# The last feed-forward in pairs of tiles, laid between the attention's steps, with its normalisations on GpSimd

## The reference

```
x += tanh(g) * masked_attention(x_normalised, ctx)            # layer 0, stage A
x += tanh(g) * quantised_gated_ffn(x_normalised)              # layer 0, stage B
q, k, v = h @ Wq.T + bq, ctx @ Wk.T + bk, ctx @ Wv.T + bv     # layer 1, stage C, 16 heads
probs   = softmax(where(mask, clip(q k / 4, -50, 50), -10000 then clipped))
delta   = residual_scale * ((probs v) @ Wo.T + bo)
x      += tanh(g) * (layernorm(delta) * gamma + beta)
x      += tanh(g) * ((silu(h @ Wgate.T) * (h @ Wup.T)) @ Wdown.T)   # layer 1, stage D, 1024 hidden
```

## Time and profile before

| | |
|---|---|
| median of three runs | 264.27 us |
| profiled execution, its own time | 264.11 us |
| span of its instructions | 262.3 us |
| PE, DVE, ACT, POOL busy | 212.0, 181.0, 132.8, 83.9 us |
| stage C from about 127 us, stage D alone from about 196 us | |

### The profile page before, as it was taken

The page is one execution under the profiler, slowest core; times in us unless marked ns, Lnnn a source line. Parts: engine busy times, 40 slices in busy tenths (PEclk is TensorE's granted clock), DMA queues, the critical chain, the costliest instruction groups (busy, mean ns, idle before and its releaser), DMA issues.

```text
span 262.3 us, 4538 instructions
## 1 busy us (share of the span) xinstructions
PE 212.0 (81%) x1658; PEld 174.5 (67%) x1658; DVE 181.0 (69%) x457; ACT 132.8 (51%) x296; POOL 83.9 (32%) x108
## 2 busy tenths in 40 slices
PE   0285557979889889897798688775999999999992
PEld 0264325858778778786576466654877888888882
DVE  2769879598988988786428999998984333262333
ACT  1138874478667667679755455553322323222220
POOL 2301111175856856868505333442100000000000
PEclk9999955699999999999959999997999999999999
DMA  5999003900000000000000000000000000020002
GB/s 169 369 390 301 5 0 139 343 1 0 2 0 0 2 1 0 2 2 0 0 2 2 0 2 4 0 4 0 2 2 0 0 0 2 0 80 2 0 0 80
DMA packets 9238, 12.55 MB, mean 48 GB/s; under 512 B 1025, under 2 KB 7937, under 8 KB 9217
## 3 DMA queue, kind: packets, MB, share of 16 engines
q1 hardware_dynamic: 8784, 12.07, 13.3%
q10 hardware_dynamic: 432, 0.20, 0.4%
HBM read 11.22 MB, written 1.05 MB: 47 GB/s over the span
## 4 chain that ended last, share of the span: by engine, by line
PE 50%; DVE 27%; ACT 7%; DMA 6%; issue 4%; POOL 3%; SPq 1%; DVEq 0%; ACTq 0%; POOLq 0%
PE PB L1259 16%; PE PB L1278 7%; DMA WRAW<-w_dram 6%; PE PB L1073 6%; PE PB L1172 4%; PE PB L1085 3%; DVE XV L524 3%; PE PB L1108 2%; PE PB L1112 2%; DVE HBQ L742 2%; PE PB L1019 2%; DVE RD L728 2%; DVE HBQ L572 2%; ACT SIL L906 2%; DVE HSD L578 2%
## 5 line engine op out<-in xcount | busy, mean ns | idle before, releaser
L1259 PE MATMUL PB<-SGN,WHI 128*128 128x512 f32 x128 | 40.5, 397 | 0.0
L1073 PE MATMUL PB<-SGN,XQH 128*128 128x512 f32 x64 | 27.7, 433 | 1.3 <-DVE XQL L553 1.3
L699 DVE TENSOR_TENSOR WRAW<-WRAW,PB 128x512 f32<-128x512 f32 x16 | 11.0, 686 | 24.0 <-ACT WRAW L993 23.9
L1278 PE MATMUL PB<-WHI,SGN 128*128 128x256 f32 x128 | 25.6, 283 | 2.2 <-DVE SGN L707 1.8
L1073 PE MATMUL PB<-SGN,XQL 128*128 128x512 f32 x64 | 27.1, 424 | 0.0
L289 POOL TENSOR_TENSOR RSTD<-MVS,MHALF 128x1 f32<-128x1 f32 x24 | 13.4, 560 | 40.9 <-DVE MVS L401 40.9
L1259 PEld LDWEIGHTS PB<-SGN,WHI 128*128 128x128 f32 x128 | 22.9, 188 | 4.5 <-issue 0.2
L1259 PE MATMUL PB<-SGN,WLO 128*128 128x512 f32 x64 | 25.2, 394 | 0.0
L993 ACT ACTIVATE WRAW<-PB 128x512 f32<-128x512 f32 x16 | 9.6, 600 | 28.0 <-PE PB L1259 28.0
L1278 PEld LDWEIGHTS PB<-WHI,SGN 128*128 128x128 f32 x128 | 20.7, 188 | 3.6 <-DVE SGN L707 2.4
L316 POOL TENSOR_TENSOR HBQ<-HBQ,HR 128x512 f32<-128x512 f32 x16 | 17.6, 1098 | 17.2 <-DVE HR L590 17.2
(11 more groups left out here) (122 smaller groups left out, 545.7 us busy)
## 6 DMA issues: line engine op xcount, KB each, us to landing
WRAW<-w_dram SPq DMA_DIRECT2D x2, 2048.0 KB, 12.1
X<-x_dram SPq DMA_DIRECT2D x2, 512.0 KB, 5.8
CTXT<-ctxt_dram SPq DMA_DIRECT2D x1, 1024.0 KB, 9.6
CTX<-ctx_dram SPq DMA_DIRECT2D x1, 1024.0 KB, 12.0
WRAW<-w_dram SPq DMA_DIRECT2D x1, 1024.0 KB, 14.9
...
```

What stands on the lines that cost most here:

```text
L1073: mm = nc.tensor.matmul(PB[2 * half + m][:], part[:, p, c, :], sgn(m, c, a, b), start=(c == 0 and k == 0), stop=(c == DC - 1 and k == 1))
L1259: mm = nc.tensor.matmul(PB[2 * b + m][:], wcol(w_part, m, c, j), act_part[:, c, g * TG:(g + 1) * TG], start=(c == 0 and i == 0), stop=(c = ...
L1278: mm = nc.tensor.matmul(down_bank(g, k), act_part[:, b, ts], wdown(w_part, j), start=(j == 0 and i == 0 and k % 2 == 0), stop=(j == FC - 1 ...
```

## The change

The last feed-forward now works on pairs of tiles (TG = 256), which gives four groups of eight chunks: 32 chunks n, each half as wide. Four of them (SPT) stand in each step of `step_c`, from chunk n = 4t - 14 on, so steps 3 to 7 hold chunks 0 to 17 beside attention, and steps 8 to 11 the rest. A chunk's gate and up halves share one bank (PB6). From chunk 17 on PB0 and PB6 alternate. Four buffers hold chunks between `gate_up_d` and `down_d`. PB5 takes the head sums, the head values and the product with Wo, PB4 also takes the transposes of XD, and PB7 gathers the result of a group, added to X by one instruction for both tiles. ScalarE takes the exponentials of tile t + 1 in step t, and in steps 3 to 6 it changes its table to exponential and back. On VectorE the mean and variance of DL move to the head of the following step, and the head values are waited for before the reciprocal. GpSimd takes over both normalisations (`norm_c`, `norm_d`). The output's transfers wait for the new semaphore `d_x`.

```
 HPC = P // HD
-TG = 512
-NG = NT * P // TG
-TPG = TG // P
+TPG = 2
+TG = TPG * P
+NG = NT // TPG
+NB = 4
+SPT = NG * FC // NT
+LEAD = 14
+LAST = (LEAD + NG * FC) // SPT + 1
 
...
-        def down_bank(g, k):
-            return PB[(4, 6)[g % 2] + k // 2][:, (k % 2) * D:(k % 2 + 1) * D]
+        def gu_bank(n):
+
+            return PB[6] if n <= SPT * NT // 2 or n % 2 == 0 else PB[0]
+
+        def ffn(n):
+
+            return 0 <= n < NG * FC
...
+            def norm_c(t, p):
+                n = t + 2 * NT
+                pool.wait_ge(xt_done, n - 1)
+                pool.wait_ge(rstd_ready, n - NT + 3)
+                nc.gpsimd.tensor_scalar(XH[:, p, :], X[:, t, :], MVS[:, t:t + 1, 0],
+                                        RSTD[:, t:t + 1], ALU.subtract, ALU.mult
+                                        ).then_inc(ln_done, 1)
+
+            def norm_d(u):
+                need(pool, d_t, u)
+                pool.wait_ge(rstd_ready, u + 2 * NT + 3)
+                nc.gpsimd.tensor_scalar(XD[:], X[:, u, :], MVS[:, u:u + 1, 0], RSTD[:, u:u + 1],
+                                        ALU.subtract, ALU.mult).then_inc(d_ln, 1)
+
             def step_c(t, p):
                 if live(t - 2):
+                    pool.wait_ge(c_ve, t - 1)
+                    nc.gpsimd.tensor_tensor(RSTD2[:], VE2[:], MHALF[:], ALU.pow
+                                            ).then_inc(c_r2, 1)
                     rstd(t - 2, t - 2 + 2 * NT)
+                    norm_d(t - 2)
+                if live(t + 2):
+                    norm_c(t + 2, p)
                 if live(t + 1):
                     v_tile(t + 1, 1 - p)
                 if live(t):
...
-                    pool.wait_ge(c_ve, t)
...
+
+                dve.wait_ge(d_dn, FC * (g + 1))
+                xs = X[:, TPG * g:TPG * (g + 1), :].rearrange("p t d -> p (t d)")
+                nc.vector.scalar_tensor_tensor(
+                    out=xs, in0=PB[7][:], scalar=TANHG[:, 3:4], in1=xs, op0=ALU.mult,
+                    op1=ALU.add).then_inc(d_x, 1)
...
+                n = SPT * t - LEAD
+                if live(t - 2):
+                    dve.wait_ge(c_de, t - 1)
+                    nc.vector.bn_stats(ST2[:], DL[:]).then_inc(c_st, 1)
...
+                if n > FC and (n - 2) % FC == 0:
+                    update_d((n - 2) // FC - 1)
+                if live(t - 2):
+                    nc.vector.scalar_tensor_tensor(
+                        out=D2[:], in0=DL[:], scalar=MV2[:, 0:1], in1=GAM[:],
+                        op0=ALU.subtract, op1=ALU.mult).then_inc(c_d2, 1)
+                if ffn(n - 1):
+                    gu_d(n - 1)
...
+                    nc.vector.scalar_tensor_tensor(
+                        out=X[:, t - 2, :], in0=D2[:], scalar=RSTD2[:], in1=X[:, t - 2, :],
+                        op0=ALU.mult, op1=ALU.add).then_inc(x_done, 1)
+                    stats(t - 2, p, t - 2 + 2 * NT)
+                if ffn(n - 1):
+                    lo_gu(n - 1)
+                if ffn(n):
+                    gu_d(n)
+                if ffn(n):
+                    lo_gu(n)
+                if live(t - 2):
+                    lo_d(t - 2)
+                if ffn(n + 1):
...
+                if live(t - 1):
+                    dve.wait_ge(c_pv, t)
...
-                    norm_d(t - 2)
+                if ffn(n + 1):
+                    lo_gu(n + 1)
+                if ffn(n + 2):
+                    gu_d(n + 2)
                 if live(t):
 
...
             def step_c(t, p):
-                if live(t):
-                    exp_c(t, p, 0)
-                    exp_c(t, p, 1)
+                n = SPT * t - LEAD
+                switch = ffn(n + 3) and live(t + 1)
                 if live(t + 1):
                     q_out(t + 1)
-                if live(t):
-                    exp_c(t, p, 2)
-                    exp_c(t, p, 3)
+                if ffn(n):
+                    silu_d(n)
+                    hi_gu(n)
+                if live(t - 2):
+                    hi_d(t - 2)
+                if ffn(n + 1):
+                    silu_d(n + 1)
+                    hi_gu(n + 1)
+                if switch and not ffn(n + 2 - SPT):
+                    warm(ACT.Silu)
+                if ffn(n + 2):
+                    silu_d(n + 2)
+                if switch:
+                    warm(ACT.Exp)
+                if live(t + 1):
+                    exp_c(t + 1, 1 - p, 0)
+                if ffn(n + 2):
+                    hi_gu(n + 2)
+                if live(t + 1):
+                    exp_c(t + 1, 1 - p, 1)
                 if live(t + 2):
                     copy_ht(t + 2, p, 4, xt_done, c_q, c_ht, 2 * NT)
-                if live(t - 2):
-                    hi_d(t - 2)
+                if live(t + 1):
+                    exp_c(t + 1, 1 - p, 2)
+                    exp_c(t + 1, 1 - p, 3)
+                if switch:
+                    warm(ACT.Silu)
+                if ffn(n + 3):
+                    silu_d(n + 3)
+                    hi_gu(n + 3)
 
             warm(ACT.Exp)
             copy_ht(1, 1, 4, xt_done, c_q, c_ht, 2 * NT)
-            pipeline(step_c, lag=0)
...
+            def gate_up_d(n):
+
+                g, j = n // FC, n % FC
+                if j == 0:
+                    pe.wait_ge(d_hl, TPG * (g + 1))
+                if n == SPT * NT // 2 + 1:
+                    pe.wait_ge(c_ex, 4 * NT)
+                elif n > SPT * NT // 2:
+                    pe.wait_ge(d_g, n - 1)
+                else:
+                    need(pe, d_g, n)
...
             def step_c(t, p):
+                n = SPT * t - LEAD
+                if t < NT and ffn(n - 3):
+                    down_d(n - 3)
                 if live(t + 1):
                     q(t + 1, 1 - p)
-                if t == NT:
-
-                    pe.wait_ge(c_ex, 4 * NT)
-                    gate_up_d(0)
                 if t == 1:
                     pe.wait_ge(b_hl, 2 * NT)
...
+                if t < NT and ffn(n - 2):
+                    down_d(n - 2)
+                if t == NT:
+                    down_d(n - 3)
+                if ffn(n):
+                    gate_up_d(n)
+                if t >= NT:
+                    down_d(n - 2)
+                if live(t - 1):
+                    head_sums(t - 1, 1 - p)
+                    if not ffn(n):
+                        head_values(t - 1, 1 - p)
+                if live(t - 2):
+                    xd_t(t - 2)
+                if ffn(n + 1):
+                    gate_up_d(n + 1)
+                if live(t - 1) and ffn(n):
+                    head_values(t - 1, 1 - p)
+                if ffn(n - 1):
+                    down_d(n - 1)
+                if ffn(n + 2):
+                    gate_up_d(n + 2)
                 if live(t + 1):
...
+                if t >= NT:
+                    down_d(n)
+                if ffn(n + 3):
+                    gate_up_d(n + 3)
+                if live(t - 1):
+                    delta(t - 1)
+                if t < NT and ffn(n):
+                    down_d(n)
+                if t >= NT:
+                    down_d(n + 1)
```

More of the change, by code:

```diff
@@ L725, in step_c @@
             def step_c(t, p):
[L726 to L731 removed]
+                n = SPT * t - LEAD
+                if live(t - 2):
+                    dve.wait_ge(c_de, t - 1)
+                    nc.vector.bn_stats(ST2[:], DL[:]).then_inc(c_st, 1)
+                    dve.wait_ge(c_st, t - 1)
+                    nc.vector.bn_aggr(MV2[:], ST2[:]).then_inc(c_mv, 1)
+                    dve.wait_ge(c_mv, t - 1)
+                    nc.vector.tensor_scalar(VE2[:], MV2[:, 1:2], LN_EPS, None, ALU.add
+                                            ).then_inc(c_ve, 1)
@@ L999, in _ @@
-            warm(ACT.Silu)
-            silu_d(0)
-            hi_gu(0)
-            hi_d(NT - 2)
-            silu_d(1)
-            hi_gu(1)
-            for n in range(2, NG * FC):
-                silu_d(n)
-                hi_gu(n)
-                if n == 2:
-                    hi_d(NT - 1)
+            for b in range(4):
+                exp_c(0, 0, b)
+            for t in range(LAST):
+                step_c(t, t % 2)
         @block.tensor
@@ L1153, in xt_c @@
                 need(pe, c_qm, 4 * t)
+                need(pe, d_hl, t - 3)
                 transpose_x(XH[:, p, :], 4, xt_done)
@@ L1163, in q, with heads @@
                 mm.then_inc(c_q, 1)
-            def heads(bank, parts, p):
+            def heads(at, parts, p):
                 for c in range(DC):
@@ L1192, in scores, with head_sums, head_values, delta @@
                             mm.then_inc(c_s, 1)
+            def head_sums(u, p):
+                pe.wait_ge(c_p, u + 1)
+                need(pe, c_de, u)
+                heads(0, lambda h: ONE2[:, h % 2, :], p)
+            def head_values(u, p):
+                pe.wait_ge(c_v, 2 * u + 2)
+                heads(D, lambda h: V1[:, p, h, :], p).then_inc(c_pv, 1)
+            def delta(u):
+                pe.wait_ge(c_o, u + 1)
```

(34 more changed lines are left out.)

185 lines of the change are left out of this document (37 added, 148 removed).

## The result

The changed kernel takes 274.5 us (median of four runs, 272.21 to 275.88) against 264.37 (four runs, 264.17 to 264.83), a ratio of 1.037 with a 95% interval of 1.030 to 1.045. The forecast was 265.3, its range ended at 271.0. The profiled execution was the fastest of the four, 272.21 us with a span of 270.3.

What follows compares the result with a forecast made beforehand. VectorE was taken to bound stage C, TensorE stage D. Followed along TensorE, gate_up(14) starts at 208.2 and TensorE ends at 258.15; tail and time outside the span give 263.4, the clock's 1.9 gives 265.3 us, range 260.3 to 271.

Steps and rivals of the forecast that it cites:

- the first DL: Start of the early steps' first DL on VectorE: 140.87 us in the kernel before, forecast 0.5 sooner, at 140.4.
- XD on GpSimd: Normalising XD on GpSimd in each step: taken as 0.72 us with 0.07 to start, bounds 0.32 and 1.09.
- the two early turns: Steps before the first chunk, where VectorE waits for a loop over four engines: 9.65 us a turn against 7.20.
- The rest of a step: TensorE from a step's third-chunk gate_up to the end of the third gate_up: 7.25 us plus 0.3 waiting for XD.
- ScalarE's run: ScalarE's SiLU, two table loads, exponentials and copies, plus VectorE's product, between two chunks of a full step: 7.0 us.
- Steps 8 and 9: TensorE stalls because XD(6) and XD(7) come late, with little work ahead of their transposes: 1.4 and 2.4 us.
- The clock: TensorE's pauses in new steps 2 and 3 bring the lower clock level: 1.9 us added, ends 0 and 3.1.
- rival 3: Each ScalarE table change costs 1.38 us more, for a drain: 277.7 us in all, chance 0.03.
- rival 4: Chunks wait for ScalarE's exponentials each step, so the last feed-forward is hardly hidden: 281 us, chance 0.02.
- the tail: After TensorE's end: a last addition of 0.8 us, 2.6 for the transfer, and 1.81 outside the span.
- Rival 1: XD on GpSimd is short, below 0.6 us, and the clock stays up: 260.9 us, chance 0.33.
- Rival 2: GpSimd and VectorE hold each other up, 0.6 us for each of eight XD: 270.1 us, chance 0.17.

Runs made afterwards that it cites:

- both on VectorE: The changed kernel with both normalisations (XD and XH) moved from GpSimd back to VectorE: 267.91 us, ratio 1.012 to the kernel before.
- the filled kernel: The changed kernel with products nobody reads put into TensorE's pauses in steps 0 to 3: 272.35 us, ratio 1.032 to the kernel before.

## Why the prediction was wrong

The mechanism was right: an early loss that TensorE must earn back, over the stretches that were named. The sign was right too, by little more than luck: the forecast lay 0.9 us above the kernel before, with a chance of 0.51 for slower. Its sizes were off by 9.2 us between the medians. In the profiled execution, which is 6.9 above the forecast, two terms were too small, XD by 3.7 in all and TensorE's own work by some 3.8, while the first DL came 1.2 earlier than forecast. The other 2.3 lie between that execution and the median.

**XD on GpSimd, the term that failed.** "XD on GpSimd: no row shows a tensor_scalar there ... I take 0.72", with an upper bound of 1.09. It measured 1.22, and the gap ahead of it 0.18 where 0.07 was taken. It counts as the forecast said: 1.2 in the two early turns, 1.1 in the full steps, where TensorE waited 0.69, 0.70 and 0.58 for it in place of 0.3 each, and 1.4 behind them. Taking XD back to VectorE shortens the loop by more than that error. From GpSimd's inverse root to the transposes it is 155.38 - 153.37 = 2.01 after and 1.18 with both on VectorE, so 0.83. At the forecast's own rate, 3.0 us for 0.37, that is 6.7, and the chip gave 5.0 to 6.6. The rate was about right, the price was not. What remains of the miss, 267.9 against 265.3, is not XD's. It is more than it looks, since the way over XD is then 1.18 where the forecast had 1.42: at the same rate that hides another 2 us, an estimate.

**TensorE's own work, the second term.** "The rest of a step ... 7.25" was 7.88 after and 7.86 with both on VectorE. Gate_ups and downs, priced from rows in which they stand beside each other, came out 0.12 to 0.22 short each beside attention's products. Three steps of 0.63 are 1.9 of the 3.4 us by which that stretch was late, the waits for XD 1.1, and ScalarE's run, 0.1 longer in each step, most of the rest.

**Steps 8 and 9.** Stalls of 1.4 and 2.4 were forecast, 1.83 and 3.00 came. With XD's extra 0.5 in each they are right within 0.1. The forecast counted two downs between gate_up(14) and down(14), where there is one, and one too few behind, which changes no sum. In the third stretch XD's two waits are 1.0, and the wait of 0.71 in step 7 is 0.4 more than forecast. TensorE's longer groups are left for most of the other 1.9, which no experiment measured by itself.

**The clock.** 1.9 us was about right for the profiled run, where the comparison with the filled kernel gives 1.7. That gate_up(2) started so near to the forecast, at 167.07 against 166.8, is luck all the same: XD had added 1.2 us by then, and the first DL had come 1.2 early. The profiled run was the fastest of four, and the median lies 2.3 higher. Filling the pauses took 1.5 to 2.2 away from it, so the clock is the likely cause of that too, but none of the longer executions was traced. The forecast took one profiled execution of before as a measure for a kernel with longer pauses, whose runs spread more: 3.7 us, where it had counted on telling half a microsecond.

**What held.** ScalarE's run with two table changes (7.0 forecast, 7.11), the table load without a drain (against rival 3), the overlap as such (against rival 4), the tail (5.2). Rival 1 fell with XD's length: its point of decision, 0.6, was passed twofold. Rival 2's sign, L381 over 1.2, came true to the letter, and its sum of 270.1 is the nearest to the profiled execution, but for another reason: all eight XD took 1.223 to 1.226 us, in the early turns and in the full steps alike, and XD moved in the kernel before took 1.23 where VectorE's XH did not run beside it. XD was not held up, it is that slow alone. Rival 3's 277.7 is nearest to the median, by chance, since its drain did not show.
